# Four gathers moved in one block behind GpSimd's last rotation, and their additions behind the last heads

## The reference

```python
q = (x @ wq).reshape(B, T, H, Dh)            # 16 heads of 128
c_kv = x @ w_down                            # 128 latent columns
kv_up = (c_kv @ w_up).reshape(B, T, H, 2 * Dh)
k, v = (kv_up[..., :Dh], kv_up[..., Dh:])
q, k = _apply_rope(q, 0), _apply_rope(k, 0)
scores = where(causal, einsum('bqhd,bkhd->bhqk', q, k) * scale, -inf)
attn = softmax(scores)
out = einsum('bhqk,bkhd->bqhd', attn, v).reshape(B, T, H * Dh) @ wo
...
combine = 2.5 * (the two largest sigmoid(xt @ gate_w.T), divided by their sum)
y = einsum('eth,ehd->etd', silu(h) * u, w2)  # 8 experts, 176 hidden
routed = einsum('etd,te->td', y, combine)
shared = silu(xt @ sw1) * (xt @ sw3) @ sw2
```

## Time and profile before

| | us |
|---|---|
| median of 3 runs (lowest, highest) | 808.88 (807.58, 812.69) |
| time of the profiled execution | 806.7 |
| its span, from its first to its last instruction | 804.9 |
| TensorE busy in it | 717.0 |
| VectorE, ScalarE, GpSimd busy | 606.6, 594.3, 578.1 |

### The profile page before, as it was taken

How to read it: one execution, slowest core, us unless ns; L and a number is a source line. 1 busy time by engine, 2 the same in 40 slices (tenths; PEclk the granted TensorE clock), 3 DMA queues, 4 the chain that set the end, 5 groups by cost and what they waited for, 6 DMA issues and landing times.

```text
span 804.9 us, 15351 instructions
## 1 busy us (share of the span) xinstructions
PE 717.0 (89%) x4538; PEld 643.0 (80%) x4538; DVE 606.6 (75%) x1675; ACT 594.3 (74%) x1466; POOL 578.1 (72%) x476
## 2 busy tenths in 40 slices
PE   3678659999899998999999999999999999999471
PEld 2567547887788887999999999999999999998461
DVE  6446778777777776888788878888788878888375
ACT  3467447877787777888888888888888888888330
POOL 2456438889889886777777777777777777778863
PEclk9788779999999999999999999999999999999775
DMA  6036133243222005554455554444455544420234
GB/s 220 27 116 213 59 117 115 91 138 116 75 86 98 27 28 160 187 148 131 139 187 151 151 150 156 151 151 132 132 191 151 152 140 134 137 77 1 59 118 138
DMA packets 62066, 99.60 MB, mean 124 GB/s; under 512 B 9840, under 2 KB 34464, under 8 KB 61984
## 3 DMA queue, kind: packets, MB, share of 16 engines
q1 hardware_dynamic: 58912, 90.22, 36.3%
q0 software_dynamic: 3072, 8.39, 3.2%
HBM read 72.12 MB, written 26.48 MB: 122 GB/s over the span
## 4 chain that ended last, share of the span: by engine, by line
PE 60%; POOL 21%; issue 7%; ACT 5%; DVE 4%; DMA 2%; SPq 0%; POOLq 0%; DVEq 0%; ACTq 0%
PE qk_proj L388 12%; PE u_acc L388 11%; PE scores L388 10%; PE ffn L388 9%; PE out_acc L388 7%; PE probs_t L495 6%; POOL rot L864 5%; POOL swapped L856 5%; POOL xs_sorted L880 4%; POOL qk_lo L871 3%; ACT qk_hi L714 1%; POOL xn L894 1%; PE ffn L572 1%; PE ffn L547 1%; ACT swapped L705 1%
## 5 line engine op out<-in xcount | busy, mean ns | idle before, releaser
L871 POOL TENSOR_TENSOR qk_lo<-rot,qk_hi 128x512 fp32r<-128x512 f32 x128 | 165.5, 1293 | 160.8 <-ACT qk_hi L714 160.8
L1098 DVE TENSOR_TENSOR pt_lo<-probs_t,pt_hi 128x512 fp32r<-128x512 f32 (+3 forms) x256 | 124.9, 488 | 69.3 <-ACT pt_hi L736 64.8
L864 POOL TENSOR_TENSOR rot<-rot,swapped 128x512 f32<-128x512 f32 x128 | 166.4, 1300 | 9.2
L856 POOL TENSOR_TENSOR swapped<-swapped,sin_t 128x512 f32<-128x512 f32 x128 | 166.2, 1299 | 1.0 <-ACT swapped L705 0.6
L736 ACT ACTIVATE pt_hi<-probs_t 128x512 fp32r<-128x512 f32 (+3 forms) x256 | 111.4, 435 | 74.6 <-PE probs_t L495 73.7
L705 ACT ACTIVATE swapped<-qk_proj 64x512 f32<-64x512 f32 x256 | 151.7, 593 | 11.9 <-PE qk_proj L388 7.5
L1083 DVE CUSTOM_DVE_ANT_0 scores<-scores,mask 128x512 f32<-128x512 f32 (+3 forms) x256 | 126.3, 493 | 28.2 <-PE scores L388 27.4
L495 PE MATMUL probs_t<-ident,probs 128*128 128x128 f32 x640 | 117.3, 283 | 25.9 <-DVE pt_lo L1098 25.9
L725 ACT ACTIVATE probs<-scores,nbias 128x512 f32<-128x512 f32 (+3 forms) x256 | 134.2, 525 | 8.2 <-DVE nbias L1083 7.2
L495 PEld LDWEIGHTS probs_t<-ident,probs 128*128 128x128 f32 x640 | 79.6, 144 | 44.7 <-issue 29.6
L1075 DVE TENSOR_TENSOR rot<-qk_proj,cos_t 128x512 f32<-128x512 f32 x128 | 87.8, 686 | 34.7 <-ACT swapped L705 34.6
(11 more groups left out here) (174 smaller groups left out, 1771.8 us busy)
## 6 DMA issues: line engine op xcount, KB each, us to landing
wt<-expert_parts SPq DMA_DIRECT2D x39, 704.0 KB, 4.4
wt<-expert_parts SPq DMA_DIRECT2D x39, 512.0 KB, 4.2
raw_a<-in_attn SPq DMA_DIRECT2D x8, 768.0 KB, 5.2
xs_sorted<-g SPq DMA_DIRECT2D x3, 1664.0 KB, 6.8
xs<-xs_sorted SPq DMA_DIRECT2D x39, 128.0 KB, 3.6
ys_sorted<-ysb SPq DMA_DIRECT2D x39, 128.0 KB, 4.0
expert_parts<-split SPq DMA_DIRECT2D x16, 304.0 KB
expert_parts<-raw_f SPq DMA_DIRECT2D x16, 304.0 KB
```

What stands on the lines that cost most here:

```text
L856: pool.tensor_tensor(swapped[:, which, :], swapped[:, which, :], sin_t[:, :], ALU.mult).then_inc(sinm_ok[which], 1)
L864: pool.tensor_tensor(rot[:, which, :], rot[:, which, :], swapped[:, which, :], ALU.add).then_inc(rot_ok[which], 1)
L871: pool.tensor_tensor(qk_lo[:, m % 2, which, :], rot[:, which, :], f32(qk_hi[:, m % 2, which, :]), ALU.subtract).then_inc(rlo_ok[which], 1)
L1098: ve.tensor_tensor(pt_lo[:, c], pt_bank[:, 0:n], f32(pt_hi[:, c]), ALU.subtract).then_inc(ptlo_ok, 1)
```

## The change

On GpSimd the four gathers stand together at step 61 (`GATHER_AT + 2`), which is the first step without a rotation. On VectorE add_routed(0) and add_routed(1) stand at the end of step 63, and add_routed(2) and add_routed(3) at the end of step 64. The waits inside `gather` and `add_routed` are the same as before. Nothing is added or left out, and the instructions of the other engines are unchanged.

```diff
@@ GpSimd's loop
-                if s >= GATHER_AT and s - GATHER_AT < B:
-                    gather(s - GATHER_AT)
+                if s == GATHER_AT + 2:
+                    for b in range(B):
+                        gather(b)
@@ VectorE's loop
-                if s > GATHER_AT + 1 and s - GATHER_AT - 2 < B:
-                    add_routed(s - GATHER_AT - 2)
+                if s > GATHER_AT + 3 and s - GATHER_AT - 2 < B:
+                    if s == SLOTS - 1:
+                        add_routed(0)
+                        add_routed(1)
+                    else:
+                        add_routed(2)
+                        add_routed(3)
```

## The result

The changed kernel has a median of 825.69 us over 4 runs (819.64 to 827.08), the kernel before in the same measurement 810.79 over 4 (807.58 to 812.74): a ratio of 1.0191, interval 1.0163 to 1.022. It is slower by 1.9%, and the forecast of 810.6 us (806 to 816) was wrong.

What follows compares the result with a forecast made beforehand. The prediction questioned only the last 61 us, ended by GpSimd's gathers waiting for VectorE's additions: add_routed(0)'s end at 777.2 plus 29.4 gave a span of 806.6, 1.7 more; 808.9 + 1.7 = 810.6 us, range 806.0 to 816.0.

Steps and rivals of the forecast that it cites:

- The hole of step 60: TensorE's 10.19 us stop before the scores of piece 63, forecast to go, starting those scores 9.9 us earlier.
- T: Start of piece 63's transposes on TensorE, forecast at 761.0 where it was 774.23, 13.2 us regained.
- T to the first half of head 63: Stretch from piece 63's transposes to head 63's first addition, forecast at 12.0 us, halfway between 9.8 and 14.2.
- The tail of 29.4: From add_routed(0)'s end at 777.2 through two gathers, last addition and store to the span's end: 29.4 us.
- rival (a): gather(2)'s issue on GpSimd is held by add_routed(1) for its whole 3.26 us; span 809.6, time 813.6; chance 0.06.
- The sum, +1.7: Forecast span of 806.6 us, 1.7 more than before.
- What lies beside this chain and costs nothing: gather(0) and gather(1), issued from about 753.2 beside the last heads, land in time and don't queue: no cost.
- Rival (d): TensorE at half clock from piece 63's transposes on; span 811.4, time 815.4 us; chance 0.09.
- rival (b): An unbroken run of GpSimd issues slows by 0.63 us each, 9.5 more; span 816.1, time 820.1; chance 0.07.

Runs made afterwards that it cites:

- A: Chip or state met in the first measurement and job 3; changed kernel against the one before: ratios 1.0191 and 1.0133.
- after_again: Changed kernel measured again without any edit, in job 1: 805.99 us, ratio 1.0018 to the kernel before.
- B: Chip or state met in jobs 1, 2, 4 and 5; changed kernel 805.99, 806.55 and 808.89 us (one run), not run in job 4.
- the five: Five traces of the kernel before, unedited; first scores of piece 62 on TensorE to span end: 60.7, 58.9, 60.3, 60.4, 60.4 us.
- apart: Changed kernel with head 63's second half added between add_routed(0) and add_routed(1), not behind both: 804.53 us, ratio 1.0024.
- add_early: Changed kernel with add_routed(0) at the end of step 62, add_routed(1) of step 63, the other two at 64: 812.97 us, ratio 1.0063.
- hold: Changed kernel with no gather before the last head's matmuls are done and all four additions at step 64: 820.9 us, ratio 1.0219.
- spaced: Changed kernel with a 1.3 us GpSimd product and a wait behind each of the first sixteen issues: 826.14 us, ratio 1.0266.
- before_own: Kernel before, order unchanged, with own buffers for gather(2)'s and gather(3)'s second choices: 801.34 us, ratio 0.997; again 801.81, 0.9974.

## Why the prediction was wrong

By its own steps, with the first trace (A) and after_again (B):

- **The hole of step 60 goes, the scores of piece 63 start at 753.3**: right, 753.35 on A. On B they start 8.6 us behind the scores of piece 62 (740.20 to 748.82), where the forecast had 9.1.
- **T, 7.7 us behind the scores**: 7.8 on B (748.82 to 756.65). On A 14.3 (753.35 to 767.63).
- **T to the first half of head 63, 12.0 us**: 10.2 on B, near the 9.8 of full clock. On A 20.7 (767.63 to 788.36).
- **The tail of 29.4**: 31.8 on both (771.12 to 802.9; 792.60 to 824.4). The 2.8 us by which gather(2)'s first issue exceeds an ordinary one are rival (a), to which I had given 0.06; the trace of before had both a scatter that was held and a gather that wasn't, and I chose the gather. The runs agree here with what the prediction quoted of the Trainium skill (SBUF — State Buffer, section "SBUF: two separate sides") at gather(2)'s first issue, and disagree with it where issues pass beside the same additions (apart).
- **The sum, +1.7**: on B the length rose from 60.4 (median of the five) to 62.7, by 2.3. T to head 63 had been priced 1.8 too dear and the tail 2.4 too cheap, and these nearly cancel: that the ratios of 1.0018 and 1.0049 lie close to the forecast's +0.2% is luck in part. What held there is the path: the hole of step 60 goes, and two gathers follow the first addition.
- **The step that failed** is the one that priced the gathers beside the heads at nothing: "What lies beside this chain and costs nothing: gather(0) and gather(1) are issued from about 753.2 ...". I had asked whether they land in time and whether their transfers queue, not whether the heads beside them would still run at their pace. On A they did not: TensorE's increments come 2.3 to 7.2 us late while the run of issues lasts. T is 6.6 us late by it, and head 63 another 8.7 by the second late increment and the half clock around it: 15.4 in all (788.36 - 773.0). With the 2.4 of the tail that is the 17.8 by which the span of 824.4 missed the 806.6.

None of the rivals had this. Rival (d) priced the half clock at 4.8 us, as a cause by itself; it came as a consequence of waits.

For rival (a) I had also read too few rows. The trace of before has 32 scatter issues. The nine that start while the subtraction of L1128 runs on VectorE take 1.37 to 1.59 us, and eight of them end 0.88 us behind it, as gather(2)'s first issue ends 0.8 behind the additions. The other 23 take 0.96 to 1.01, also where the subtraction starts just behind the issue, as here (GpSimd, then VectorE, kernel before):

```profile
136.75 1.01 POOL L880 DMA_INDIRECT xs_sorted<-xn,place  x1 [0.15 <-issue]
...
137.03 0.79 DVE L1128 TENSOR_TENSOR raw_f<-raw_f,split 128x608 fp32r<-128x608 f32 x1 [0.40 <-ACT split L697]
```

**What is shown and what isn't.** Shown: the late increments, in three traces of two kernels on A, and in none of the 16 traces of seven kernels on B; and that on A they, with the half clock around them, make up 15.4 of the 17.8 us. Shown too: they don't need the moved additions (add_early). Not shown is what makes them late. All three traces have the unbroken run of sixteen gathers beside heads 61 to 63, and in the first the lateness begins and ends within some us of it, which argues for the run as its cause; but the same run stands in the traces of the changed kernel on B without it. No trace of hold, spaced or apart was taken on A, and none of the kernel before that I know to be A's. The kernel before took 808.1 us on A and about 804 on B: whether those 4 us are a lesser form of the same is open. So is what distinguishes A.

Whether the profile's recording has a part in it is open as well. The three traces on A lack some 550 to 640 of about 9,790 semaphore records, and they lack them where GpSimd's indirect DMAs are issued: of the 256 records of the transfers of gather(0) and gather(1), the first trace has 53. Missing records alone don't make a kernel slow, as there are missing ones beside the scatters too, and the steps keep their pace there: from the step that starts near 75 us to the one near 324 the first trace takes 248.8 us and after_again 248.7. The ratios of 1.0191 and 1.0133 can't rule it out, because every timed execution has a span and a granted clock in the record, so each of them was recorded in some form.

## What to carry to other kernels

Moving work that "waits for nothing" into a stretch is not free because its own data arrive in time: ask what runs beside it there, and give a chance to a case that no row of before can show. Before a rival gets its chance, read all rows of its kind, not one: here nine of 32 scatters spoke for it. Where buffers couple an early step to a late one, separate the buffers before moving the work: before_own, a few changed lines, was the only version measured faster than before in two jobs, if only by 0.3%. Time a change of this size in more than one job, the kernel before beside it in each, and compare traces from a common instruction on, not by their spans.

## What the runs showed of the hardware

- On A ScalarE got TensorE's increments 6.5 and 7.3 us after the matmuls' ends (VectorE one 2.3 us after), with two stops of TensorE of 6.5 us each as a result; on B the same kernel shows none.
- The same changed kernel is 0.2 and 0.5% slower than the one before in two jobs, and 1.3 and 1.9% in two others.
- An indirect DMA's issue of 0.95 us took 3.72 and 3.26 beside VectorE's additions with both operands in SBUF, and 0.95 to 1.28 beside others of them. Nine scatter issues that start within a VectorE subtraction of two SBUF operands take 1.37 to 1.59, the other 23 0.96 to 1.01 (before). The other way round, four such additions took 4.92 and 5.18 us in place of 1.67 beside GpSimd's products of 1.27 to 1.30 (spaced), which lost nothing.
- Sixteen indirect DMAs of 128 rows are issued back to back at 1.25 us each without slowing (753.23 to 772.09 in the first trace after): rival (b) is out.
